# Order of the bank moves, interleaved row ranges and a second DMA queue in a fused attention schedule

## The chip, the cores and the metric

The program runs on one core of one Trainium2 chip. It is a whole decoder of twelve sub-layers in one launch; the metric is the device time of that launch in microseconds. The core's engines are PE (TensorE, matrix products into PSUM), DVE (VectorE), ACT (ScalarE), POOL (GpSimd) and SP (SyncE, which here only issues DMAs). Each runs its own instruction stream in order, and semaphores tie the streams together.

## The reference

Only one of the twelve sub-layers matters here, the fourth layer's attention. It handles 16 batches of 128 rows, width 128, 16 heads of 8, and has two attentions one after the other: each batch over itself, then its output over two fixed sets of 256 past states, which all batches share.

```python
q, k, v = (_split_heads(_lin(hidden_states, W, b)) for W, b in ((Wq, bq), (Wk, bk), (Wv, bv)))
attn = softmax(einsum('bhsd,bhtd->bhst', q, k) * SCALE)
output = _lin(_merge_heads(einsum('bhst,bhtd->bhsd', attn, v)), Wo, bo)
rq = _split_heads(_lin(output, Wrq, brq))
rk = _split_heads(_lin(past_states, Wrk, brk)); rv = _split_heads(_lin(past_states, Wrv, brv))
rattn = softmax(einsum('bhsd,pbhtd->pbhst', rq, rk) * SCALE)
recursive_output = _merge_heads(einsum('pbhst,pbhtd->pbhsd', rattn, rv)).mean(axis=0)
gate = sigmoid(_lin(concatenate([output, recursive_output]), Wg, bg))
return output * (1 - gate) + recursive_output * gate      # then x = layernorm(x + this)
```

All of it is computed in fp32; a fp32 product is two passes on PE, and the trace has one record for each pass.

## The kernel before

`l3_attn` (from line 810) holds the stage. The 16 batches are cut into four groups of `G = 4`, so that a tile is 128 partitions by 512 columns (4 batches by 128). Heads have only 8 rows, so queries and keys of four heads lie in one tile at partitions 0, 32, 64 and 96 (`ROW = 32`), in four such sets (`SETS = 4`). Projections give a dense tile (`dense_q`, `dense_k`, `dense_rk`), and `spread_rows` (line 908) copies its 16 heads of 8 rows, one DMA each, to their places; all these DMAs are issued by SP, in the order of its stream: parameter loads first, then four for `b_rq4`, eight that zero rows of `rk4`, then for each task of kind `q`, `k` or `rk` a wait for its move and 16 copies.

The order of the work is written out by hand in **slots**. A group has 40 (`PER`), and functions say what slot t holds:

- `a_at(t)`: two heads of **scores** (rows are queries), whose maximum DVE takes (`peak`). Slots 8 to 15 of a group hold self scores of the next group (L960, four 128-column products a head, 8 passes), the others past scores (L967, one 512-column product, 2 passes).
- `b_at(t)`: two heads of **turned scores** (rows are keys), 11 slots later, with the maximum folded in as an extra row; ACT takes their exponential (`exp`, L1092). Self ones are L982, past ones L990.
- `o_at(t)`: in every second slot the **values** of four heads, L1004 and L1009, which go to four column ranges of bank 6.
- `misc_at(t)`: at most one **extra task**, always in bank 7, named by a key: `x` and `pt` (turn the input), `q`, `k`, `v`, `rk`, `rv` (projections), `mt` and `rmt` (turn the maxima), `ot` and `rot` (turn the sums for the division), `o2`, `out`, `rq` (output projection and next queries), `rec`, `gate`, `fin` (combine, gate, residual).

PE's stream goes through the slots: a, b, o, misc. Scores use banks 0 to 2 in turn, turned scores banks 3 to 5. `score` (line 941) waits with `pe.wait_ge(maxed, n - 2)` before head n, that is for the reduction of head n - 3; `turned_score` (line 969) waits likewise on `exped`. Each handles one head; for a self head it runs its four batches one after the other in one 32-row range. `other(key)` waits until the previous task's bank has been moved (`moved`).

ACT and DVE each move some kinds of tasks (`ON_ACT` lists ACT's). In slot t both do this, with `exp` on ACT and `peak` on DVE:

```python
two, before = b_at(t), misc_at(t - 1)
if two:
    exp(two[0])
if before is not None and before[0] in ON_ACT:
    evacuate(before)
if two:
    exp(two[1])
```

so the move of the task of slot t - 1 stands between slot t's two exponentials (reductions). Behind them ACT copies a finished sum (`move_sum`, L1099) and scales the result four slots after `fin` (`apply`, L1137); DVE has `blend` after `gate` (L1200 to L1202) and `moments` two slots after `fin` (L1207, L1211). POOL clears tiles, waits for all 15 parameter loads, spreads `w_rq4`, and then computes the layer norm's `rstd` for each group. The first `q` task on PE waits for all 15 loads too.

Since the first scores need queries and keys of group 0 and nothing else can run yet, the stage starts with a stretch that has few tasks in flight (slots -40 to -1); slots 0 to 10 have scores but no turned scores.

## Time and profile before

| | us |
|---|---|
| median of the runs (6590.18 to 6593.02, 3 runs) | 6592.16 |
| the profiled execution | 6582.25 |
| its span, first to last instruction | 6580.5 |
| this stage in it, about 5282 to 5891 | 609 |
| busy in the span: PE 4913.6, DVE 4375.5, ACT 2893.6, POOL 2329.9 | |

A time of a row is the start in the profiled span, then the length. Matmuls are pipelined: a group's busy time reaches from its first start to its last end, and the next group may start a little before that end. The profile gives PE's granted clock as a share of 2.4 GHz: 1.00 is 2.4 GHz, 0.50 is 1.2 GHz. Slots don't appear in the profile; they are found by counting the passes of L960 and L967 in order.

### The profile page before, as it was taken

The numbers are of one execution on the slowest core, as the hardware profiler recorded it, in microseconds if no ns is written. First come the engines' busy times: TensorE is split into PE (matmuls) and PEld (weight loads), VectorE is DVE, ScalarE is ACT, GpSimd is POOL, SyncE is SP. The second block draws the span as 40 slices with busy tenths as digits, with TensorE's granted clock in tenths as the row PEclk, the third lists the DMA queues.
The fourth block names the chain that finished last, engine by engine and source line by source line (L and its number), as shares of the span: only waits on it lengthen the run. The fifth ranks groups of instructions, "written<-read, shape, count | busy, mean of one in ns | idle before, by whom it ended". The sixth has DMA issues, their size and how long they took to land. (4 is left out here: it accounts for less than half of the span.)

```text
span 6580.5 us, 86052 instructions
## 1 busy us (share of the span) xinstructions
PE 4913.6 (75%) x27787; PEld 2961.6 (45%) x27787; DVE 4375.5 (66%) x8424; ACT 2893.6 (44%) x4778; POOL 2329.9 (35%) x2032
## 2 busy tenths in 40 slices
PE   6645799999999999676731667666687678863667
PEld 4534466666666666324521222222465354422434
DVE  4522788888888888474446699999554335538635
ACT  2211577777777776452211455454232314432311
POOL 0011666666666666241011466666100200000100
PEclk8755999999999999787765899999898869985878
DMA  0000100000000000000000000000000000002000
GB/s 13 0 4 0 32 1 18 1 18 1 18 1 18 1 4 1 4 0 2 2 0 0 7 0 0 0 1 0 12 0 12 0 15 5 3 10 54 6 21 6
DMA packets 72547, 48.55 MB, mean 7 GB/s; under 512 B 26672, under 2 KB 66761, under 8 KB 71433
## 3 DMA queue, kind: packets, MB, share of 16 engines
q1 hardware_dynamic: 72201, 44.17, 2.7%
q8 instruction: 189, 3.10, 0.2%
q14 instruction: 157, 1.29, 0.1%
HBM read 39.53 MB, written 1.18 MB: 6 GB/s over the span
## 5 line engine op out<-in xcount | busy, mean ns | idle before, releaser
L2942 POOL TENSOR_TENSOR l_attn_read<-l_attn_state,l_attn_c_rows 128x1024 f32<-128x1024 f32 x256 | 604.4, 2361 | 328.7 <-DVE l_attn_state L2845 327.8
L1828 POOL TENSOR_TENSOR l_ffn_t<-l_ffn_t 128x512 f32<-128x512 f32 x384 | 488.7, 1273 | 593.7 <-DVE l_ffn_t L1696 593.7
L2845 DVE TENSOR_TENSOR_SCAN l_attn_state<-l_attn_decay,psum 128x1024 f32<-128x1024 f32 x256 | 584.9, 2285 | 8.0
L203 POOL TENSOR_SCALAR rstd<-mean_var 128x4 f32<-128x4 f32 (+1 forms) x36 | 8.4, 232 | 1621.4 <-DVE mean_var L192 1621.4
L1428 PE MATMUL psum<-l_ffn_wq,l_ffn_xsT 128*128 128x512 f32 x1152 | 563.2, 597 | 21.9 <-DVE l_ffn_t L1696 13.2
L2647 PE MATMUL psum<-l_attn_read,ident 128*128 128x512 f32 x1024 | 493.9, 605 | 5.4 <-DVE l_attn_yz L2853 3.0
L2638 PE MATMUL psum<-l_attn_parts,pick 96*128 96x512 bf16 x512 | 199.9, 393 | 311.1 <-DVE psum L2837 311.1
L1839 POOL TENSOR_TENSOR l_ffn_p<-l_ffn_p,l_ffn_sm 128x512 f32<-128x512 f32 x384 | 399.8, 1041 | 63.4 <-DVE l_ffn_sm L1728 46.8
L1834 POOL TENSOR_TENSOR l_ffn_t<-l_ffn_t,l_ffn_ss 128x512 f32<-128x512 f32 x384 | 401.0, 1044 | 0.7 <-DVE l_ffn_ss L1711 0.7
L2764 ACT COPY l_attn_c_rows<-psum 128x512 f32<-128x512 f32 x256 | 149.9, 586 | 467.8 <-PE psum L2638 467.7
L1593 ACT COPY l_ffn_pT<-psum 128x512 f32<-128x512 f32 x384 | 224.6, 585 | 271.3 <-PE psum L1458 267.8
L2837 DVE TENSOR_TENSOR psum<-psum,l_attn_du 128x1024 f32<-128x1024 f32 x256 | 315.6, 1233 | 31.7 <-POOL l_attn_du L2919 4.6
L1692 DVE TENSOR_TENSOR l_ffn_t<-psum,l_ffn_tab 128x512 f32<-128x512 f32 x384 | 263.2, 685 | 105.9 <-ACT l_ffn_sq L1576 104.1
L1092 ACT ACTIVATE l_attn_pT<-psum 128x512 f32<-128x512 f32 x320 | 178.3, 596 | 299.2 <-PE psum L990 205.2
L1587 ACT ACTIVATE l_ffn_p<-l_ffn_p 128x512 f32<-128x512 f32 x384 | 241.4, 629 | 150.3 <-DVE l_ffn_p L1719 148.0
L1715 DVE TENSOR_REDUCE l_ffn_mx<-psum 128x4 f32<-128x512 f32 x384 | 257.7, 671 | 73.4 <-PE psum L1449 72.4
L2638 PEld LDWEIGHTS psum<-l_attn_parts,pick 96*128 96x128 bf16 x512 | 49.8, 98 | 555.5 <-DVE psum L2837 483.0
L2757 ACT ACTIVATE l_attn_decay<-l_attn_dt,l_attn_a 128x1016 f32<-128x1016 f32 x256 | 292.8, 1144 | 12.4 <-DVE l_attn_state L2845 12.1
L1472 PEld LDWEIGHTS psum<-l_ffn_pT,l_ffn_v 128*64 128x64 f32 x3072 | 160.1, 136 | 280.2 <-issue 173.8
L1576 ACT ACTIVATE l_ffn_sq<-psum 128x512 f32<-128x512 f32 x384 | 230.6, 601 | 117.0 <-PE psum L1428 117.0
L1173 DVE TENSOR_REDUCE l_attn_rtop<-psum 128x2 f32<-128x512 f32 x256 | 168.7, 685 | 169.8 <-PE psum L967 169.6
L1449 PE MATMUL psum<-l_ffn_kT,l_ffn_qT 64*128 64x128 f32 x3072 | 274.7, 297 | 0.0
(762 smaller groups left out, 12273.6 us busy)
## 6 DMA issues: line engine op xcount, KB each, us to landing
l_ffn_wq<-in_L_ffn_Wqkv SPq DMA_DIRECT2D x6, 1536.0 KB, 6.1
l_xattn_toep<-s4d_taps SPq DMA_DIRECT2D x4, 2048.0 KB, 17.5
l_ffn_wo<-in_L_ffn_Wo SPq DMA_DIRECT2D x6, 512.0 KB, 7.7
l_ffn_w<-in_L_ffn_W SPq DMA_DIRECT2D x6, 341.0 KB
l_ffn_w<-in_L_ffn_w SPq DMA_DIRECT2D x3, 512.0 KB, 5.6
l_attn_q<-l_attn_dense_q SPq DMA_DIRECT2D x64, 16.0 KB
l_attn_k<-l_attn_dense_k SPq DMA_DIRECT2D x64, 16.0 KB
l_xattn_conv_y<-l_xattn_conv_rows SPq DMA_DIRECT2D x64, 16.0 KB, 2.2
```

The costliest lines, as they stand in the source:

```text
L1428: nc.tensor.matmul(ring[it % 2], xsT[:, n % 2, m % G, :], wq[:, z, i * 512:(i + 1) * 512], start=True, stop=True).then_inc(itemed, 1)
L1449: last = nc.tensor.matmul(S[:, par, i, :], qT[r, m % G, 2 * c + i, :], kT[r, m % G, 2 * c + i, :], start=False, stop=True, skip_group_chec ...
L1692: nc.vector.tensor_tensor(t1[:, m % G, i, :].rearrange("p (h d) -> p h d", d=dh), dots.rearrange("p (h d) -> p h d", d=dh), rows(tab[:, z, ...
L1715: nc.vector.reduce_max(mx[:, k % 2, :, :], S, AX).then_inc(max_found, 1)
L1828: nc.gpsimd.tensor_tensor(t1[:, m % G, i, :], t1[:, m % G, i, :], t2[:, x % 3, :], ALU.add).then_inc(added, 1)
L1834: nc.gpsimd.tensor_tensor(t1[:, m % G, i, :].rearrange("p (h d) -> p h d", d=dh), t1[:, m % G, i, :].rearrange("p (h d) -> p h d", d=dh), ...
L1839: nc.gpsimd.tensor_tensor(p_[:, k % 4, :, :], p_[:, k % 4, :, :], col(sm[:, k % 4, :], T), ALU.mult).then_inc(weighted, 1)
L2647: last = nc.tensor.matmul(total[:, h * GT:(h + 1) * GT], K.ident[:], read[:, k % 3, h * GT:(h + 1) * GT], start=(n == 0), stop=(n == N - 1 ...
L2757: nc.scalar.activation(decay[:, k % 3, :, :, 1:T], dt[:, g % 2, :].rearrange("p (h g t) -> p h g t", h=2, g=G)[:, :, :, 1:T], ACT.Exp, sca ...
L2837: nc.vector.tensor_tensor(drive.rearrange("p (h n) -> p h n", h=2), rows(b_bank, 2), du[:, g % 2, :].rearrange("p (h n) -> p h n", h=2), A ...
L2845: nc.vector.tensor_tensor_scan(state[:, k % 3, :], decay[:, k % 3, :, :, :].rearrange("p h g t -> p (h g t)"), drive, 0.0, ALU.mult, ALU.a ...
L2942: nc.gpsimd.tensor_tensor(read[:, k % 3, :].rearrange("p (h n) -> p h n", h=2), state[:, k % 3, :].rearrange("p (h n) -> p h n", h=2), row ...
```

## The change

1. In ACT's and DVE's slots the move of the previous slot's task comes first, ahead of both exponentials or reductions.
2. `score` and `turned_score` take both heads of the slot. They wait for both banks first. For self heads the loop over batches is outside and the loop over the two heads (two row ranges, two banks) inside.
3. Weights and biases of q and k are loaded first, on a semaphore `qk_in` of their own, for which the first q task waits; the wait for the other 11 loads moves to the `rk` task.
4. The 16 copies of a `k` task are issued by POOL instead of SP. POOL's stream goes through the slots, too: for group 0 the copies stand ahead of the `w_rq4` spread, for the others at the slot of their task, between the `rstd` computations.

```diff
-            N_LOAD = 15
+            N_LOAD = 11
+            def spread_rows(eng, dst, src, sem):
+                for s in range(SETS):
+                    for j in range(4):
+                        h = 4 * j + s
+                        eng.dma_start(dst[ROW * j:ROW * j + dh, s, :], src[dh * h:dh * h + dh, :]).then_inc(sem, 16)
...
-                    for n in ("q", "k", "v", "rk", "rv", "o", "rq"):
+                    for n in ("q", "k"):
+                        sp.dma_start(w[n][:], I[pre + "W" + n]).then_inc(qk_in, 16)
+                        sp.dma_start(bias[n][:], column(I[pre + "b" + n])).then_inc(qk_in, 16)
+                    for n in ("rk", "v", "rv", "o", "rq"):
                         sp.dma_start(w[n][:], I[pre + "W" + n]).then_inc(loaded, 16)
...
-                    if key[0] == "k":
-                        spread_rows(k4, stage_k, k_set)
...
-                def score(key):
-                    n = a_use[key]
-                    if n >= 3:
-                        pe.wait_ge(maxed, n - 2)
+                def score(keys):
+                    for key in keys:
+                        n = a_use[key]
+                        if n >= 3:
+                            pe.wait_ge(maxed, n - 2)
...
                         for b in range(G):
                             at = slice(b * T, b * T + T)
-                            last = nc.tensor.matmul(ps[:, at], q4[r, s, at], k4[r, s, at], start=True, stop=True)
+                            for j in (j0, j0 + 1):
+                                r = slice(ROW * j, ROW * j + ROW)
+                                ps = K.bank[a_use["self", g, s, j] % 3]
+                                last = nc.tensor.matmul(ps[:, at], q4[r, s, at], k4[r, s, at], start=True, stop=True)
+                                if b == G - 1:
+                                    last.then_inc(a_done, 1)
...
                     if kind == "q":
                         if g == 0:
-                            pe.wait_ge(loaded, 16 * N_LOAD)
+                            pe.wait_ge(qk_in, 64)
...
                     if kind == "rk":
+                        pe.wait_ge(loaded, 16 * N_LOAD)
...
                     two, before = b_at(t), misc_at(t - 1)
-                    if two:
-                        exp(two[0])
                     if before is not None and before[0] in ON_ACT:
...
                         evacuate(before)
-                    if two:
-                        exp(two[1])
+                    for key in two:
+                        exp(key)
...
+                def spread_k(key):
+                    pool.wait_ge(moved, use[key] + 1)
+                    spread_rows(nc.gpsimd, k4, stage_k, k_set)
...
+                pool.wait_ge(cleared, 2)
+                spread_k(("k", 0))
+                pool.wait_ge(loaded, 16 * N_LOAD)
+                pool.wait_ge(rq_bias, 64)
...
+                for t in slots:
+                    key, done = misc_at(t), misc_at(t - 2)
+                    if key is not None and key[0] == "k" and key[1] > 0:
+                        spread_k(key)
+                    if done is not None and done[0] == "fin":
+                        rstd_of(done[1])
```

`turned_score` is changed as `score` is, and DVE's slots as ACT's.

## Rows read from the trace of the kernel before

**Rows 1.** By stretch: length, busy PE, PEld, DVE, ACT, POOL (instructions), PEclk, DMA, GB/s.

```profile
5554.00:5678.00 124.00, 107.93 (x916) 55.66 (x917) 65.84 (x125) 58.06 (x110) 1.67 (x4) 1.00 0.03 5
...
5400.00:5440.00 40.00, 40.00 (x193) 27.27 (x191) 17.77 (x27) 5.43 (x10) 0.00 (x0) 0.50 0.00 1
5441.00:5812.00 371.00, 325.94 (x2642) 158.96 (x2634) 195.61 (x374) 174.15 (x325) 3.42 (x9) 1.00 0.02 4
```

**Rows 2.** Timeline of an odd slot with task rq: PE, then ACT.

```profile
5625.48 0.70 PE L967 MATMUL psum<-l_attn_rk,l_attn_rq 32*128 32x512 f32 x2
...
5627.95 1.12 PE L1059 MATMUL psum<-l_attn_outT,l_attn_w_rq 128*128 128x512 f32 x2 [1.33 <-ACT l_attn_rq L1119]
5629.01 0.70 PE L967 MATMUL psum<-l_attn_rk,l_attn_rq 32*128 32x512 f32 x2
...
5626.72 0.60 ACT L1092 ACTIVATE l_attn_pT<-psum 128x512 f32<-128x512 f32 x1 [1.39 <-PE psum L990]
5627.22 0.68 ACT L1119 ACTIVATE l_attn_rq<-psum,l_attn_b_rq 128x512 f32<-128x512 f32 x1
```

**Rows 3.** Timeline of PE, the even slot before it.

```profile
5621.95 0.70 PE L967 MATMUL psum<-l_attn_rk,l_attn_rq 32*128 32x512 f32 x2
...
5623.02 1.06 PE L1009 MATMUL psum<-l_attn_pT,l_attn_rv 128*32 128x512 f32 x8
5624.42 1.12 PE L1059 MATMUL psum<-l_attn_outT,l_attn_w_rq 128*128 128x512 f32 x2 [0.34 <-ACT l_attn_rq L1119]
```

**Rows 4.** Timeline of PE, an odd and an even slot without a task.

```profile
5519.05 0.70 PE L967 MATMUL psum<-l_attn_rk,l_attn_rq 32*128 32x512 f32 x2
...
5520.96 0.70 PE L990 MATMUL psum<-l_attn_rq,l_attn_rk 32*128 32x512 f32 x2
...
5522.02 1.06 PE L1009 MATMUL psum<-l_attn_pT,l_attn_rv 128*32 128x512 f32 x8
5523.02 0.70 PE L967 MATMUL psum<-l_attn_rk,l_attn_rq 32*128 32x512 f32 x2
```

**Rows 5.** Timeline of PE, a slot with self scores; and self values.

```profile
5541.59 1.37 PE L960 MATMUL psum<-l_attn_k,l_attn_q 32*128 32x128 f32 x13
5542.70 0.70 PE L990 MATMUL psum<-l_attn_rq,l_attn_rk 32*128 32x512 f32 x2
...
5543.75 1.07 PE L1009 MATMUL psum<-l_attn_pT,l_attn_rv 128*32 128x512 f32 x8
...
5377.87 1.08 PE L1004 MATMUL psum<-l_attn_pT,l_attn_v 128*32 128x128 f32 x32
```

**Rows 6.** Timeline of PE: a task of four turns, and rec.

```profile
5589.04 0.66 PE L1015 MATMUL psum<-ident,l_attn_rtop 128*128 128x128 f32 x4 [0.67 <-DVE l_attn_o L1195]
...
5556.76 2.05 PE L1063 MATMUL psum<-ident,l_attn_ro 128*128 128x128 f32 x16 [0.36 <-DVE l_attn_q L1184]
```

**Rows 7.** Timeline of the start: copies issued by SP, and the first scores.

```profile
5296.55 10.71 SPq L913 DMA_DIRECT2D l_attn_q<-l_attn_dense_q  x16
5307.31 11.04 SPq L913 DMA_DIRECT2D l_attn_k<-l_attn_dense_k  x16
...
5319.83 9.18 PE L960 MATMUL psum<-l_attn_k,l_attn_q 32*128 32x128 f32 x64 [13.53 <-DMA l_attn_k<-l_attn_dense_k]
```

**Rows 8.** Timeline of PE: first scores of slots 12, 16, 56, 80 and 96.

```profile
5418.63 0.58 PE L960 MATMUL psum<-l_attn_k,l_attn_q 32*128 32x128 f32 x1
...
5438.48 1.22 PE L967 MATMUL psum<-l_attn_rk,l_attn_rq 32*128 32x512 f32 x2
...
5554.26 0.70 PE L967 MATMUL psum<-l_attn_rk,l_attn_rq 32*128 32x512 f32 x2
...
5635.51 0.70 PE L967 MATMUL psum<-l_attn_rk,l_attn_rq 32*128 32x512 f32 x2
...
5677.54 0.70 PE L967 MATMUL psum<-l_attn_rk,l_attn_rq 32*128 32x512 f32 x2
```

**Rows 9.** Timeline of DVE, slots with scores alone.

```profile
5394.64 2.60 DVE L1173 TENSOR_REDUCE l_attn_rtop<-psum 128x2 f32<-128x512 f32 x4 [11.22 <-PE psum L967]
```

More of the change, by code:

```diff
@@ L897, in l3_attn @@
         ON_ACT = ("x", "q", "k", "rq", "pt", "rk", "o2", "out", "rec", "gate", "fin")
-        names = ("past_in", "loaded", "spread", "cleared", "clear_step", "zeroed", "filled", "moved", "q_set", "k_set", "rk_set", "rq_bias",
+        names = ("past_in", "qk_in", "loaded", "spread", "cleared", "clear_step", "zeroed", "filled", "moved", "q_set", "k_set", "rk_set", "rq_bias",
                  "a_done", "maxed", "b_done", "exped", "o_done", "o_moved", "recip", "mix_step", "mixed", "stats_step", "var_ready", "rstd_step",
@@ L959, in score @@
                             at = slice(b * T, b * T + T)
-                            last = nc.tensor.matmul(ps[:, at], q4[r, s, at], k4[r, s, at], start=True, stop=True)
-                    else:
-                        _, g, s, b, j = key
-                        r = slice(ROW * j, ROW * j + ROW)
-                        if b == j == 0:
-                            pe.wait_ge(moved, use["rq", g, s] + 1)
-                            pe.wait_ge(rk_set, 256)
-                        last = nc.tensor.matmul(ps, rq4[r, g % 2, s, b * T:b * T + T], rk4[r, s, :], start=True, stop=True)
@@ L968, in score @@
-                    last.then_inc(a_done, 1)
-                def turned_score(key):
-                    n = b_use[key]
-                    if n >= 3:
-                        pe.wait_ge(exped, n - 2)
-                    ps = K.bank[3 + n % 3]
-                    if key[0] == "self":
-                        _, g, s, j = key
-                        r = slice(ROW * j, ROW * j + ROW)
-                        if j == 0:
+                            for j in (j0, j0 + 1):
[4 more added lines that the diff above has]
+                                    last.then_inc(a_done, 1)
+                    else:
+                        for key in keys:
+                            _, g, s, b, j = key
+                            r = slice(ROW * j, ROW * j + ROW)
+                            if b == j == 0:
+                                pe.wait_ge(moved, use["rq", g, s] + 1)
+                                pe.wait_ge(rk_set, 256)
+                            nc.tensor.matmul(K.bank[a_use[key] % 3], rq4[r, g % 2, s, b * T:b * T + T], rk4[r, s, :],
+                                             start=True, stop=True).then_inc(a_done, 1)
@@ L979, in turned_score @@
+                def turned_score(keys):
+                    for key in keys:
+                        n = b_use[key]
+                        if n >= 3:
+                            pe.wait_ge(exped, n - 2)
+                    if keys[0][0] == "self":
+                        _, g, s, j0 = keys[0]
+                        if j0 == 0:
                             pe.wait_ge(moved, use["mt", g, s] + 1)
@@ L981, in turned_score @@
                             at = slice(b * T, b * T + T)
-                            last = nc.tensor.matmul(ps[:, at], k4[r, s, at], q10[r, s, at], start=True, stop=True)
-                    else:
-                        _, g, s, p, kb, j = key
-                        r = slice(ROW * j, ROW * j + ROW)
-                        if p == kb == j == 0:
-                            pe.wait_ge(moved, use["rmt", g, s] + 1)
-                            pe.wait_ge(zeroed, 128)
-                        at = (2 * p + kb) * T
-                        last = nc.tensor.matmul(ps, rk4[r, s, at:at + T], rq10[r, s, :], start=True, stop=True)
-                    last.then_inc(b_done, 1)
+                            for j in (j0, j0 + 1):
+                                r = slice(ROW * j, ROW * j + ROW)
+                                ps = K.bank[3 + b_use["self", g, s, j] % 3]
+                                last = nc.tensor.matmul(ps[:, at], k4[r, s, at], q10[r, s, at], start=True, stop=True)
+                                if b == G - 1:
+                                    last.then_inc(b_done, 1)
+                    else:
+                        for key in keys:
+                            _, g, s, p, kb, j = key
+                            r = slice(ROW * j, ROW * j + ROW)
+                            if p == kb == j == 0:
+                                pe.wait_ge(moved, use["rmt", g, s] + 1)
+                                pe.wait_ge(zeroed, 128)
+                            at = (2 * p + kb) * T
+                            nc.tensor.matmul(K.bank[3 + b_use[key] % 3], rk4[r, s, at:at + T], rq10[r, s, :], start=True, stop=True).then_inc(b_done, 1)
                 def value(key):
@@ L1075, in _ @@
                 for t in slots:
-                    for key in a_at(t):
-                        score(key)
-                    for key in b_at(t):
-                        turned_score(key)
+                    if a_at(t):
+                        score(a_at(t))
+                    if b_at(t):
+                        turned_score(b_at(t))
                     if o_at(t) is not None:
@@ L1219, in _ @@
                     two, before = a_at(t), misc_at(t - 1)
-                    if two:
-                        peak(two[0])
                     if before is not None and before[0] not in ON_ACT:
                         evacuate(before)
-                    if two:
-                        peak(two[1])
+                    for key in two:
+                        peak(key)
                     if before is not None and before[0] == "gate":
```

38 lines of the change are left out of this document (14 added, 24 removed).

## The prediction

> **What bounds the kernel now.** The change touches one stage, the fourth layer's attention, about 5282 to 5891 us of a span of 6580.5. I read the busy time by stretch first [rows 1]. No engine is full: between 5554 and 5678, the 124 us in which group 1 runs in full, PE is busy 108, DVE 66 and ACT 58. So waits and PE's order decide. PE's timeline cut into slots of the hand-written schedule comes next (a slot starts with the first L967 or L960 matmul). A group has 40 slots; that one takes 5554.26 to 5677.54, 123.28 us [rows 8].
>
> An odd slot (two rows of score heads, two of turned scores, one extra task) shows the wait [rows 2]: scores start at 5625.48, the task's matmul only at 5627.95, 2.47 later, and the next slot at 5629.01. ACT explains it. It takes the first exponential at 5626.72, when the scores are ready, and only then moves the previous task's bank at 5627.22 for 0.68; the single task bank is free at 5627.90, and PE goes on at 5627.95. That bank was full 2.4 us before. PE stood idle 1.33 of this.
>
> An even slot also has values [rows 3]: scores 5621.95, values 5623.02, task 5624.42, next slot 5625.48, 3.53 in all; the values hide most of the same wait. Without a task [rows 4] the odd and even slots together take 5519.05 to 5523.02, 3.97, and another limit appears: three banks per kind. The even slot's second head waits for the odd slot's first reduction and starts at 5520.96, 1.91 after the slot before.
>
> **Part 1: the move ahead of both reductions or exponentials.** It adds and removes no instruction. Prices: from scores to another kind of matmul 1.06 (5520.96 to 5522.02), values 1.00 (5522.02 to 5523.02) [rows 4]; a task of two 512-column passes 1.06 (5627.95 to 5629.01) [rows 2]; four turns are busy 0.66 [rows 6], less the 0.07 by which the next start overlaps (as 1.12 busy against 1.06 in rows 2): 0.59; rec 1.99 likewise from 2.05 [rows 6], and gate and fin, which are as long, 1.93. The move itself is 0.68 and starts once the earlier task has drained, so it ends near 0.8 to 1.2 after the slot's start, beside the scores: at nothing on the path. What is late next: PE itself, or the three banks. So an odd slot with a task becomes the larger of 1.06 + task and 1.90; an even one 1.06 + 1.00 + task.
>
> Group 1, its first 24 slots, now 5554.26 to 5635.51 = 81.25 [rows 8]. New, odd: four with turns 4 x 1.90 = 7.6 (1.65 by PE, the banks rule); five with two passes 5 x 2.12 = 10.6; v 2.15; gate 2.99; fin 3.94 (DVE's three blend operations, 0.7 each, follow gate's move and both reductions, and fin waits for them). Sum 27.3. Even: nine with turns 9 x 2.65 = 23.9; two with passes 2 x 3.12 = 6.2; rec 4.05; 0.3 more where DVE's moments or ACT's four scalings get in front of a reduction. Sum 34.5. Together 61.8: a gain of 19.5.
>
> **Part 2: row ranges alternate.** Today a self head's eight passes run in one row range, one behind the other, at 0.11 apart: in [rows 5] L960 runs from 5541.59, and the other kind's scores, queued behind both heads, start only at 5542.70, 1.11 later; values follow at 5543.75, so 2.16 after the start. Would two ranges really run side by side? L1004 already alternates over four column ranges: 32 passes in 1.08 us [rows 5], where one range at 0.11 would need 3.5. L967 and L990 start four heads in four ranges together. So I take full overlap: the block falls by one head's 0.55, to about 1.61, wherever the bank wait isn't the limit. In the remaining 16 slots of group 1, 5635.51 to 5677.54, nine have no task, or one that hides (gain 0.2, since odd and even still add up to 3.97), and seven have the group's first kind as self scores: 5 x 0.55 + 2 x 0.81 (part 1 helps there too) = 4.4. In the eight slots where the turned scores are self scores, part 2 shortens the even slots by 0.55 each; that is already in the 2.65. Group 1: 19.5 + 0.2 + 4.4 = 24.
>
> The same prices for the 5438 to 5554 stretch (slots without rec, gate, fin): 20.6. For 5678 to 5768 (32 slots, fewer tasks as no group follows): 14.0.
>
> **The added wait.** A pair now waits for both heads' banks before either starts. Where a slot has both kinds or values this costs nothing: PE's order made the rest wait already. Where only one kind runs, the pair can't overlap the reduction before it. DVE alone now runs four reductions in 2.60 [rows 9], 1.30 a slot; the new slot is 1.90 at the full clock, and about 2.9 at half. Eight such slots at 5393 to 5405, now 11.9, become 15.2 to 19.2: I take +5. Eight with self scores at 5320 to 5343 cost about +0.65 each without a task (2.70 for 2.04) and lose as much less where a turn's wait goes: +0.1 in sum. Turned scores at 5344 to 5370 gain 1.9, the serial tasks after them 0.4, slots 8 to 15 of group 0 gain 3.2 (some 15 matmuls of it still at half clock, [rows 1], 5400 to 5440). Start region: -0.4. After 5768, one kind only: exponentials set the pace (unchanged); gate and a few tasks give 2.
>
> **Part 3: loads first, keys by POOL.** Today q's sixteen copies are issued from 5296.55, k's behind them from 5307.31, the last lands about 1.5 after its issue ended, and the first scores start at 5319.83 after 13.5 idle [rows 7]. The earlier semaphore lets q's matmul start at about 5287 instead of 5292.8, but SP still has the same loads and eight rk rows in front, so q's copies still start at 5296.55 and land by 5308.8. k's bank is moved by about 5292.9, and POOL is free by then. No row shows a copy issued by POOL. Bounds: SP's 0.67 each (10.71/16), and for the other end twice that, 1.34, as a second engine that forms each copy itself has no row here. I take 1.0, the middle: 5293 + 16 + 1.5 = 5310.4, a gain of 9.4, call it 9. At 0.67 the q copies rule: 11.1; at 1.34: 4.0. Later groups' keys have 20 slots of slack. POOL's rstd work for group g stands six slots ahead of a key spread and isn't delayed; rk's copies leave SP 11 us earlier and are needed 75 us later.
> The Trainium skill speaks partly against this ("DMA: Bandwidth & Descriptors", Issuing engines are not separate DMA queues): a second issuing engine saves only the sequencer's time, since all copies share the same DMA engines. Here SP's issue, 10.7 us for sixteen copies, is the long part, so by that rule the gain would stand too; had the transfers been the limit, the term would be 0. The same page (Latency and other measured facts) gives about 1 us to the first byte for GpSimd-issued copies; if each issue cost that, 16 us, an estimate that agrees with the middle and isn't its ground.
>
> **Sum.** -9 -0.4 -20.6 -24 -14 -2 = -70.0 us. Against the profiled execution's 6582.25: 6512. The median of the runs is 9.9 above it, 6592.16, and I subtract from that: **6522 us**.
>
> **Rivals.**
> *Second bank.* If PE in effect waits for a slot's second reduction or exponential too (moves push both back), an odd slot is not 1.90 but about 2.45. For: ACT already spends 0.68 + 0.49 + 0.60 in such a slot. Against: the wait counts name the first. About 60 odd slots x 0.45 = 27 less: 6549. 12%.
> *Alternation gives nothing.* Weight loads of two ranges queue up. Against: L1004. Costs 0.55 in some 45 slots, 24: 6546. 9%.
> *POOL slow.* 2 us a copy: keys land at 5326.5, 6.7 later than now, not 9 earlier: 6538. 9%.
> *Slower: the clock.* PE's granted clock was 0.50 in 5400 to 5440 and 1.00 from then on, with four row ranges busy [rows 1]. Should the one-kind slots with their longer pauses keep it at 1.2 GHz, each later slot costs more: four slots (12 to 15 of a group) take 5418.63 to 5438.48, 19.9 us, in group 0 at half clock [rows 8] and 5541.59 to 5554.26, 12.7, in group 1 [rows 5, 8]: 1.8 a slot. It turns the sum from the 39th such slot on; for two groups (80 slots) +144 - 70: 6666. Against: PE's pauses become shorter in every slot that had a task. 4%. In the other direction the denser slots may lift it earlier, worth up to 10.
> *Not what it says*, the bank not being the limit: then nothing moves and the one-kind slots add 5: about 6590. 2%.
>
> **How the numbers follow.** The forecast case has 64%. Its own spread: POOL -2/+5, one-kind slots and clock +/-5, slot prices 15% of 59 (+/-9): 6508 to 6540. The range reaches to the first two rivals: 6505 to 6556. A measurement of this kernel can tell about 0.2%, 13 us, from no change. Faster by more: 0.95; within: 0.02; slower: 0.03.
>
> **What would show it.** After: the group from its slot 16 to the next takes 99 us, not 123; in odd slots the task matmul follows the scores at 1.06, and ACT's move stands before the slot's first exponential; PE waits for ACT's rq hardly at all; self passes of two ranges start in pairs 0.11 apart; the first scores start near 5310; DVE's reductions at 5393 to 5405 have 0.6 gaps. The prediction is wrong if odd slots stay near 2.5, if the POOL copies take over 1.3 us each, or if the clock row of 5441 to 5812 falls below 1.00.

## Result and profile after

The changed kernel took **6533.49 us** (median of 4 runs, 6525.79 to 6540.53) against 6592.15: a ratio of 0.9914, 95% interval 0.9899 to 0.9929. The prediction was 6522, range 6505 to 6556. The profiled execution took 6532.18, its span 6530.4, 50.1 less than the span of before. The medians lie 58.7 apart: the profiled run of before was 9.9 below its median, that of after 1.3. So the steps are compared between the two profiles, by stretch.

By stretch, kernel after, from the stage's first load over slots -32, 0, 16, 56, 96, 128 and 169 to ACT's last instruction of the stage, the next stage's first load and the end (columns as in [rows 1]):

```profile
5283.48:5309.73 26.25, 12.54 (x30) 6.49 (x31) 8.67 (x8) 4.51 (x6) 14.86 (x26) 0.50 0.27 59
5309.73:5381.72 71.99, 58.04 (x446) 42.27 (x446) 15.68 (x29) 16.28 (x28) 8.00 (x16) 0.63 0.07 12
5381.72:5431.19 49.47, 41.07 (x206) 21.07 (x205) 22.60 (x35) 5.98 (x11) 0.00 (x0) 0.56 0.00 1
5431.19:5529.17 97.98, 92.58 (x879) 42.93 (x879) 63.30 (x113) 54.63 (x101) 7.95 (x16) 0.98 0.04 7
5529.17:5630.14 100.97, 96.50 (x910) 46.49 (x909) 66.62 (x125) 58.08 (x109) 9.77 (x20) 1.00 0.03 7
5630.14:5710.58 80.44, 72.92 (x678) 34.14 (x677) 52.64 (x101) 47.15 (x89) 1.67 (x4) 1.00 0.01 1
5710.58:5811.06 100.48, 84.79 (x443) 28.08 (x443) 41.48 (x80) 44.03 (x82) 1.66 (x4) 0.90 0.00 1
5811.06:5837.60 26.54, 14.52 (x66) 6.96 (x62) 4.73 (x15) 6.99 (x14) 1.66 (x4) 0.81 0.00 0
5837.60:5843.20 5.60, 0.00 (x0) 0.00 (x0) 0.00 (x0) 0.00 (x0) 0.00 (x0) 0.50 0.01 1
5843.20:6530.43 687.23, 394.62 (x2569) 259.19 (x2570) 402.52 (x1569) 155.07 (x302) 46.05 (x76) 0.74 0.10 23
```

PE is now busy 96.50 of group 1's 100.97 us; it was 107 of 123. The same cut through before, and through one of the experiments (E4, below), gives this ledger. "Predicted" is the prediction's own term.

| stretch | before | after | change | predicted | E4 |
|---|---|---|---|---|---|
| first load to slot -32 | 37.42 | 26.25 | -11.2 | -9 | 26.24 |
| slots -32 to 15 | 118.65 | 121.46 | +2.8 | -0.4 | 116.75 |
| slots 16 to 55 | 115.78 | 97.98 | -17.8 | -20.6 | 95.54 |
| slots 56 to 95 (group 1) | 123.28 | 100.97 | -22.3 | -24 | 99.53 |
| slots 96 to 127 | 91.15 | 80.44 | -10.7 | -14 | 77.50 |
| slots 128 to 168 | 97.33 | 100.48 | +3.2 | -2 | 97.33 |
| **stage to slot 169** | 583.61 | 527.58 | **-56.0** | -70.0 | 512.89 |
| slot 169 to ACT's last | 24.97 | 26.54 | +1.6 | 0 | 23.40 |
| change of stage | 2.41 | 5.60 | **+3.2** | 0 | 5.59 |
| the stages behind | 687.12 | 687.23 | +0.1 | 0 | 691.38 |
| the stages ahead | 5282.41 | 5283.48 | +1.1 | 0 | 5285.30 |

**An odd slot with rq**, timeline of PE, then ACT; it answers to [rows 2]:

```profile
5585.06 0.70 PE L973 MATMUL psum<-l_attn_rk,l_attn_rq 32*128 32x512 f32 x2
...
5586.13 1.13 PE L1070 MATMUL psum<-l_attn_outT,l_attn_w_rq 128*128 128x512 f32 x2
5587.19 0.70 PE L973 MATMUL psum<-l_attn_rk,l_attn_rq 32*128 32x512 f32 x2
...
5585.17 0.69 ACT L1130 ACTIVATE l_attn_rq<-psum,l_attn_b_rq 128x512 f32<-128x512 f32 x1 [0.42 <-PE psum L1070]
5586.30 1.08 ACT L1103 ACTIVATE l_attn_pT<-psum 128x512 f32<-128x512 f32 x2 [0.45 <-PE psum L1001]
```

The move starts 0.11 after the slot and the exponentials follow. The task comes 1.07 behind the scores, with no wait, and the slot takes 2.13 where it took 3.53.

**A slot with self scores**, PE; it answers to the first group of [rows 5]:

```profile
5612.30 0.82 PE L963 MATMUL psum<-l_attn_k,l_attn_q 32*128 32x128 f32 x10
5612.86 0.70 PE L1001 MATMUL psum<-l_attn_rq,l_attn_rk 32*128 32x512 f32 x2
...
5613.92 0.66 PE L1025 MATMUL psum<-ident,l_attn_rtop 128*128 128x128 f32 x4
5614.50 0.38 PE L963 MATMUL psum<-l_attn_k,l_attn_q 32*128 32x128 f32 x2
```

Turned scores start 0.56 after the self scores, not 1.11.

**Slots with one kind** (0 to 4), PE, then DVE; they answer to [rows 9]:

```profile
5381.72 1.13 PE L973 MATMUL psum<-l_attn_rk,l_attn_rq 32*128 32x512 f32 x4
5383.72 1.13 PE L973 MATMUL psum<-l_attn_rk,l_attn_rq 32*128 32x512 f32 x4 [0.87 <-DVE l_attn_rtop L1182]
...
5387.65 2.08 PE L973 MATMUL psum<-l_attn_rk,l_attn_rq 32*128 32x512 f32 x4 [0.84 <-DVE l_attn_rtop L1182]
5390.56 2.07 PE L973 MATMUL psum<-l_attn_rk,l_attn_rq 32*128 32x512 f32 x4 [0.83 <-DVE l_attn_rtop L1182]
...
5382.88 1.29 DVE L1182 TENSOR_REDUCE l_attn_rtop<-psum 128x2 f32<-128x512 f32 x2 [11.21 <-PE psum L973]
5384.85 1.29 DVE L1182 TENSOR_REDUCE l_attn_rtop<-psum 128x2 f32<-128x512 f32 x2 [0.68 <-PE psum L973]
```

PE and DVE take turns: each slot waits 0.85 for DVE, and DVE waits 0.68 for PE. The first slots, at 2.4 GHz, take 2.0 us, those from 5387.65 on, at 1.2 GHz, 2.91; there DVE waits 1.62.

**The start**, SP's queue, POOL and PE; it answers to [rows 7]:

```profile
5297.63 10.71 SPq L911 DMA_DIRECT2D l_attn_q<-l_attn_dense_q  x16
...
5294.60 8.25 POOL L911 DMA_DIRECT2D l_attn_k<-l_attn_dense_k  x16 [5.34 <-ACT l_attn_dense_k L1116]
...
5309.73 2.08 PE L963 MATMUL psum<-l_attn_k,l_attn_q 32*128 32x128 f32 x16 [6.70 <-DMA l_attn_q<-l_attn_dense_q]
```

POOL issues a copy in about 0.5 us (8.25/16), faster than SP in 0.67. Its last copy is issued by 5302.85 and a copy lands 1.8 us after its issue, so the keys are there by 5305 or so; the queries are now last.

### The profile page after: what moved, and what is told of

It reads as the page before. It is cut to its first block and busy times, and to the rows that moved or that the text cites. A ratio compares the mean times of both kernels' runs of the same rounds, so it can differ in the third digit from the quotient of the medians.

```text
span 6530.4 us, 86354 instructions
## 1 busy us (share of the span) xinstructions
PE 4875.4 (75%) x27785; PEld 2919.0 (45%) x27787; DVE 4377.8 (67%) x8424; ACT 2893.0 (44%) x4778; POOL 2359.2 (36%) x2096
## 5 line engine op out<-in xcount | busy, mean ns | idle before, releaser
L1448 PE MATMUL psum<-l_ffn_wq,l_ffn_xsT 128*128 128x512 f32 x1152 | 564.9, 599 | 20.5 <-DVE l_ffn_t L1716 12.0
L2777 ACT ACTIVATE l_attn_decay<-l_attn_dt,l_attn_a 128x1016 f32<-128x1016 f32 x256 | 292.8, 1144 | 11.5 <-DVE l_attn_state L2865 11.1
L2658 PEld LDWEIGHTS psum<-l_attn_parts,pick 96*128 96x128 bf16 x512 | 50.1, 98 | 552.8 <-DVE psum L2857 480.3
L1739 DVE TENSOR_TENSOR l_ffn_p<-psum,l_ffn_mx 128x512 f32<-128x512 f32 x384 | 265.4, 691 | 13.2
```

What stands on the lines that cost most here:

```text
L1448: nc.tensor.matmul(ring[it % 2], xsT[:, n % 2, m % G, :], wq[:, z, i * 512:(i + 1) * 512], start=True, stop=True).then_inc(itemed, 1)
L1739: nc.vector.tensor_tensor(p_[:, k % 4, :, :].rearrange("p (i par) t -> p par i t", par=2), S, mx[:, k % 2, :, :].unsqueeze(3).to_broadcast ...
L2777: nc.scalar.activation(decay[:, k % 3, :, :, 1:T], dt[:, g % 2, :].rearrange("p (h g t) -> p h g t", h=2, g=G)[:, :, :, 1:T], ACT.Exp, sca ...
```

## Experiments

All runs in one table; "stage" is the length from the first load to slot 169 in the profile, which compares kernels better than a total does (E11, E12).

| kernel | median us | ratio to before | 95% interval | stage |
|---|---|---|---|---|
| after | 6533.49 | 0.9914 | 0.9899 to 0.9929 | 527.6 |
| E1 moves between | 6592.32 | 1.0002 | 0.9993 to 1.0011 | 583.1 |
| E2 moves first, alone | 6546.85 | 0.9934 | 0.9921 to 0.9948 | 543.5 |
| E3 heads in series | 6567.10 | 0.9970 | 0.9959 to 0.9982 | 561.1 |
| E4 late waits | 6520.69 | 0.9892 | 0.9876 to 0.9907 | 512.9 |
| E5 keys by SP | 6552.06 | 0.9941 | 0.9928 to 0.9955 | 541.1 |
| E6 like E4, zero rows late | 6513.57 | 0.9889 | 0.9874 to 0.9904 | 502.3 |
| E7 like E6, with fillers | 6509.79 | 0.9878 | 0.9863 to 0.9893 | 505.2 |
| E8 start alone | 6585.15 | 0.9998 | 0.9989 to 1.0007 | 576.3 |
| E9 one-kind slots late | 6523.20 | 0.9902 | 0.9886 to 0.9917 | 523.7 |
| E10 like E6, half the filler | 6526.49 | 0.9912 | 0.9899 to 0.9926 | 523.1 |
| E11 before again (1 run) | 6583.90 | | | 586.8 |
| E12 after again (1 run) | 6536.49 | | | 527.6 |

### E1: alternation and start, the moves back between

```diff
-                    if before is not None and before[0] in ON_ACT:
-                        ...
-                    for key in two:
-                        exp(key)
+                    if two:
+                        exp(two[0])
+                    if before is not None and before[0] in ON_ACT:
+                        ...
+                    if two:
+                        exp(two[1])
```
(and the same on DVE)

> The changed kernel with part 1 undone: the task's move stands again between the slot's two exponentials (reductions). Pairs, alternation, early loads and POOL's key copies stay. Theory (the bank of the task is the limit): in odd slots the task matmul again follows the scores by about 2.4 us instead of 1.07, group 1 (its slot 16 to the next group's) takes about 118.5 us instead of the changed kernel's 101.0, and the time is about 6580 us. Rival (the alternation carries the gain, the moves little): group 1 below 108 us and a time near 6550.

Measured: 6592.32, no change in the total, where the theory had 6580. Group 1 takes 120.89 us, near the theory's 118.5 and far from the rival's 108. Slot 77, PE, then ACT and DVE:

```profile
5619.46 0.70 PE L973 MATMUL psum<-l_attn_rk,l_attn_rq 32*128 32x512 f32 x2
...
5621.93 1.13 PE L1070 MATMUL psum<-l_attn_outT,l_attn_w_rq 128*128 128x512 f32 x2 [1.33 <-DVE l_attn_rtop L1184]
...
5620.71 0.60 ACT L1103 ACTIVATE l_attn_pT<-psum 128x512 f32<-128x512 f32 x1 [1.39 <-PE psum L1001]
5621.20 0.68 ACT L1130 ACTIVATE l_attn_rq<-psum,l_attn_b_rq 128x512 f32<-128x512 f32 x1
...
5620.62 1.29 DVE L1184 TENSOR_REDUCE l_attn_rtop<-psum 128x2 f32<-128x512 f32 x2 [2.24 <-PE psum L973]
```

The picture of [rows 2] is back to the hundredth: task 2.47 behind the scores, 1.33 idle. (The profile names DVE, whose reductions end at 5621.91. By the code the task waits for the move alone, which ends at 5621.88; the two lie 0.03 apart.)

The total hides gains and losses. Alternation gives its 0.55 also here wherever the slot doesn't wait for the move. Slot 90, PE:

```profile
5652.34 0.83 PE L963 MATMUL psum<-l_attn_k,l_attn_q 32*128 32x128 f32 x10
5652.90 0.70 PE L1001 MATMUL psum<-l_attn_rq,l_attn_rk 32*128 32x512 f32 x2
...
5655.54 0.83 PE L963 MATMUL psum<-l_attn_k,l_attn_q 32*128 32x128 f32 x10
```

It takes 3.20 us for 3.75 in before, while slots 56 to 67, where the move decides, gain 0.5 us in all. Slots 16 to 95 together gain 4.0 us, and the start has its 11.2 us too. Against that stand 2.8 us in slots -32 to 15, 2.0 in slots 96 to 127, and 9.9 in slots 128 to 168 (107.22 for 97.33), where the granted clock was 0.84 for 0.93. So the stage ends 0.5 us shorter than before's, and the change of stage and the stages behind take 7.3 us more. Where a slot waits for the move, time saved in front of it is worth nothing; in the other slots it counts.

### E2: the moves first, alone

The kernel before with this on ACT, the same on DVE, and nothing else:

```diff
-                    if two:
-                        exp(two[0])
                     if before is not None and before[0] in ON_ACT:
                         ...
-                    if two:
-                        exp(two[1])
+                    for key in two:
+                        exp(key)
```

> The kernel before with part 1 alone: the task's move first, everything else as before. Theory: odd slots with four turns near 1.9 to 2.0, with a two-pass task near 2.15, self slots still with heads in series; group 1 about 108.5 us (before 123.3), nothing gained at the start, one-kind slots as before: about 6553 us. Rival (without the alternation the freed slots run into the three banks again): group 1 above 115 and a time above 6570.

Measured: 6546.85, 6 us below the theory. Group 1 by stretch:

```profile
5544.03:5650.52 106.49, 106.49 (x910) 56.15 (x909) 66.85 (x124) 58.58 (x109) 1.67 (x4) 1.00 0.03 6
```

That is 16.8 of the 22.3 us that group 1 gained, and 40.1 of the stage's 56.0: the largest part by far. Odd slots with turns and past scores (57, 71 and 73) take 1.66 here, not the 1.9 to 2.0 of the theory. Of the other 15.9 us of the stage the start has 11.1, so alternation and the pair waits together are worth some 4.8; with the late waits of E4 the same difference is some 19.

### E3: heads in series again

```diff
-                        for b in range(G):
-                            at = slice(b * T, b * T + T)
-                            for j in (j0, j0 + 1):
+                        for j in (j0, j0 + 1):
+                            for b in range(G):
+                                at = slice(b * T, b * T + T)
```

> The changed kernel with the two loops exchanged: a pair of self heads still waits for both banks first, but runs head after head. Theory: each slot with self scores and another kind is 0.55 us longer at the full clock (a self slot of group 1 about 2.76 and 3.75 instead of 2.21 and 3.20), one-kind self slots are not longer (2.7 to 2.9 at half clock, since the first head's reduction starts earlier), in sum +22: about 6555. Rival (alternation gives nothing): within 4 us of the changed kernel's 6533.

Measured: 6567.10, slower than the theory said. Slot 89, PE, to be laid beside the self slot of after:

```profile
5640.70 1.37 PE L963 MATMUL psum<-l_attn_k,l_attn_q 32*128 32x128 f32 x13
5641.81 0.70 PE L1001 MATMUL psum<-l_attn_rq,l_attn_rk 32*128 32x512 f32 x2
...
5643.46 0.37 PE L963 MATMUL psum<-l_attn_k,l_attn_q 32*128 32x128 f32 x1
```

1.11 again in place of 0.56, and 2.76 us for the slot in place of 2.20: the 0.55 of the prediction, so two row ranges do run side by side. The Trainium skill ("TensorEngine Tiling (Array Packing)", Key Properties) says that different tiles can run weight loads and matmuls in parallel; the trace agrees. Group 1 takes 108.47, 7.5 more than after. The slots -32 to 15 take 135.0 for 121.5. As expected, slots with self scores alone and no task are not longer (2.9 us in both kernels); but those with a task are (slots -29 and -27: 4.04 for 3.05), and so are the turned ones with a task (slot -20: 4.07 for 3.05), mostly at 1.2 GHz. That the expectation had left out. Slots 128 to 168 take 4.5 us more, with 34 us at 1.2 GHz in place of 20.5.

### E4: each wait in front of its own multiplication

```diff
-                    for key in keys:
-                        n = a_use[key]
-                        if n >= 3:
-                            pe.wait_ge(maxed, n - 2)
+                    def free(key):
+                        n = a_use[key]
+                        if n >= 3:
+                            pe.wait_ge(maxed, n - 2)
+                    ...
+                            if alone and b == 0:
+                                free(keys[j - j0])
...
                         for key in keys:
+                            free(key)
```
(`alone`: the slot holds one kind; its self heads then run in series. Self heads beside the other kind alternate and wait in pairs as in after. `turned_score` likewise)

> The changed kernel, but each past head waits for its own bank only, right ahead of its own matmul, and a self pair is alternated (with both waits first) only in slots that hold the other kind too; alone it runs head after head with its own wait. Theory (the early wait costs the one-kind slots): the eight slots from slot 0 of group 0 take about 12 us instead of 20.5, the eight self slots at the start about 2 less, the ones near the end 2 to 3 less: about 6521. Rival (the clock decides there: PE is granted half clock whenever only one kind runs, and what the waits give back it takes): 6528 to 6538, with as much time at half clock as the changed kernel.

Measured: 6520.69, the time that was expected, and better than both kernels, but in part by another way: the theory had no gain in slots 16 to 127, and these give 6.8 of the stage's 14.7 us, while the stages behind took 4.2 us more. A slot without a task and the next one, PE:

```profile
5592.44 0.70 PE L980 MATMUL psum<-l_attn_rk,l_attn_rq 32*128 32x512 f32 x2
...
5593.41 1.62 PE L980 MATMUL psum<-l_attn_rk,l_attn_rq 32*128 32x512 f32 x3
...
5596.40 0.70 PE L980 MATMUL psum<-l_attn_rk,l_attn_rq 32*128 32x512 f32 x2
```

and the same two slots in the kernel after:

```profile
5598.79 0.70 PE L973 MATMUL psum<-l_attn_rk,l_attn_rq 32*128 32x512 f32 x2
...
5600.79 0.70 PE L973 MATMUL psum<-l_attn_rk,l_attn_rq 32*128 32x512 f32 x2 [0.85 <-DVE l_attn_rtop L1182]
...
5602.97 0.70 PE L973 MATMUL psum<-l_attn_rk,l_attn_rq 32*128 32x512 f32 x2
```

In the kernel before, the first head of the even slot of [rows 4] started 0.98 after the odd slot (5519.05):

```profile
5520.03 1.62 PE L967 MATMUL psum<-l_attn_rk,l_attn_rq 32*128 32x512 f32 x3
```

With late waits it starts 0.97 after, and the two slots take 3.96; with the pair wait it starts 2.00 after and the two take 4.18. An odd slot with turns takes 1.66 instead of 2.00. The ledger's last column says what that adds up to: each of the middle stretches has, to within 0.4 us, the length that the prediction's term gave it.

### E5: the keys by SP again

```diff
+                    if key[0] == "k":
+                        sp.wait_ge(moved, use[key] + 1)
+                        spread_rows(sp, k4, stage_k, k_set)
...
-                spread_k(("k", 0))
...
-                    if key is not None and key[0] == "k" and key[1] > 0:
-                        spread_k(key)
```

> The kernel after, with the sixteen copies of group 0's keys (and the later groups') issued by SP again behind those of the queries; the earlier loads, the moves and the alternation stay. In the kernel after POOL issues a copy every 0.50 us beside SP's 0.67. Theory (the queue is what the start gains by): the keys' copies follow the queries' on one queue, sixteen times 0.67 = 10.7 us later, and the first scores with them: from the stage's first load to slot -32 about 37 us in place of 26.3, and the time about 6533 + 10.7 = 6544 us. Rival (the earlier loads give the start's gain and the queue nothing): 26 to 28 us to slot -32 and 6533 to 6535 us.

Measured: 6552.06, 8 us above the theory; slot -32 is 37.41 us behind the first load, as the theory said. SP's queue, and by stretch the start and the change of stage:

```profile
5301.37 10.71 SPq L911 DMA_DIRECT2D l_attn_q<-l_attn_dense_q  x16
5312.13 11.01 SPq L911 DMA_DIRECT2D l_attn_k<-l_attn_dense_k  x16
```

```profile
5287.21:5324.62 37.41, 12.53 (x31) 6.52 (x31) 8.67 (x8) 4.52 (x6) 6.63 (x10) 0.50 0.19 42
...
5854.90:5857.37 2.47, 0.00 (x0) 0.00 (x0) 0.00 (x0) 0.00 (x1) 0.00 (x0) 0.50 0.02 7
```

So without the second queue the earlier loads give nothing: they only let q's matmul run sooner, ahead of copies that can't start sooner. Whether the queue would give the 11.2 us without them was not run. The time above the theory is not in the start: slots -32 to -1 took 2.2 us more than in after, and the stages behind 6.6 us more (693.81), in the same code. And the second row gives a price that the prediction did not have: the change of stage takes 2.47 us here and 5.60 in after.

### E6: the zero rows behind the queries

```diff
-                for j in range(4):
-                    for p in range(2):
-                        ...
...
                         spread_rows(sp, q4, stage_q, q_set)
+                        if key[1] == 0:
+                            zero_rows()
```
(against E4; `zero_rows` holds the loop that is taken out, the eight copies into `rk4`)

> The kernel with each wait in front of its own slot's first multiplication (e4_late_waits), and the eight copies of zero rows, which SP issues ahead of the queries' copies, moved behind the first set of those. Theory (SP's queue decides when the first scores start, since they wait for the queries' copies): eight times 0.67 = 5.3 us less in front of slot -32, 21 us from the stage's first load in place of 26.3, and the time about 6520.7 - 5 = 6516 us. Rival (the copies wait for the projections and not for their queue): slot -32 where it was, and 6520 to 6521 us.

Measured: 6513.57. SP's queue and PE:

```profile
5296.04 10.84 SPq L911 DMA_DIRECT2D l_attn_q<-l_attn_dense_q  x16
...
5308.53 9.21 PE L972 MATMUL psum<-l_attn_k,l_attn_q 32*128 32x128 f32 x64 [1.73 <-DMA l_attn_q<-l_attn_dense_q]
```

Slot -32 is 21.54 us behind the first load, 4.7 earlier than in E4. Its stage of 502.3 us is the shortest of all. Of the 10.6 us that it is shorter than E4's, 4.6 lie in slots -32 to 15, whose code is the same, with 86 us at 1.2 GHz in place of 96.

### E7 and E10: fillers for the clock

E7 adds to E6, in slots -32 to 15 without a task:

```diff
+                    elif -32 <= t < 16:
+                        pe.wait_ge(moved, ...)
+                        for _ in range(2):
+                            nc.tensor.matmul(misc, K.ident16[:], K.zeros16[:], start=True, stop=True)
```

E10 has one of them instead of two, and only up to slot -1; so it changes two things against E7.

> e6_late_waits_zero_rows with two multiplications more (128 x 128 by 512 columns, 16 bit, of zeros) in every slot from -32 to 15 that has no task; nothing reads what they write. Theory (the granted clock of PE follows how densely it is used, and the slots -32 to 15 run at half of it for 60 of their 76 us because their score multiplications use little of the array): the clock is granted in full over most of these slots and they take 8 to 20 us less, 6496 to 6508 us. Rival (the clock has its own course there): the granted clock falls and rises where it did and each filler pair costs 0.4 us at full clock and 0.9 us at half, 10 to 35 us more, 6526 to 6550 us.

> e6_late_waits_zero_rows with one filler multiplication in place of two, and only in the slots -32 to -1 that have no task. In e7_filler the granted clock of PE was 1.0 from 5362 us on where e6_late_waits_zero_rows had 0.5 up to 5418 us but for two stretches, and the fillers took back what that gave. Theory (half as much filler still keeps the clock up): 1.0 from about 5362 us on, slots -32 to -22 6 us longer than without filler in place of 12, slots 8 to 15 at 18.5 us in place of 27, 6500 to 6506 us. Rival (half of it is too little, or it has to go on up to slot 15): the clock is 0.5 again in the slots 0 to 15, and the filler only costs, 6514 to 6525 us.

Slots 0 to 15 by stretch, of E6, E7 and E10:

```profile
5381.55:5420.68 39.13, 38.36 (x205) 23.91 (x205) 22.92 (x35) 5.52 (x10) 0.00 (x0) 0.61 0.00 1
```

```profile
5391.94:5424.42 32.48, 32.48 (x230) 16.14 (x229) 22.15 (x35) 5.52 (x10) 0.00 (x0) 1.00 0.00 1
```

```profile
5392.86:5434.23 41.37, 40.60 (x206) 25.35 (x205) 23.06 (x35) 5.98 (x11) 0.00 (x0) 0.57 0.00 1
```

With two fillers a slot (E7) the granted clock is 1.00 over these slots, without any (E6) 0.61, and in E10, where the single fillers end at slot -1, 0.57. So the clock follows what PE is given to do there; it doesn't have a course of its own. But the fillers cost 12.3 us in slots -32 to -22 alone (36.63 for 24.30), at 1.2 GHz, and slots -32 to 15 take 117.2 us for 112.2: the clock came as the theory said, the 8 to 20 us did not. The stage is 3 us longer than E6's, and the time, 6509.79, lies just above the theory's range and can't be told apart from E6's. (The theory's 60 of 76 us at half clock were those of slots -32 to -1 in E4.) E10's fillers cost 17.6 us up to slot 0 (90.57 for 73.02) and buy nothing: the rival's case, with 6526.49 us just above its 6514 to 6525. Whether one filler would do if it went on up to slot 15 is open.

### E8: the start alone

The kernel before with parts 3 and 4 of the change:

```diff
+                    for n in ("q", "k"):
+                        sp.dma_start(w[n][:], I[pre + "W" + n]).then_inc(qk_in, 16)
...
+                spread_k(("k", 0))
```

> The kernel before with the start's parts of the change alone: W and b of q and k loaded ahead of the rest, and the keys' copies issued by POOL. Score multiplications and moves stay as before. Theory (the start is worth 11 us by itself, and the alternation and the pair waits take back what it gives in the kernel with the moves between): from the stage's first load to slot -32 26.3 us in place of 37.4, every later stretch as before, the time 6592 - 11 = 6581 us. Rival (what comes earlier at the start is waited for later in any case, by the clock or by the tasks): 6587 to 6592 us, as in the kernel with the moves between.

Measured: slot -32 at 26.26, the 11.2 us are there; the time, 6585.15, can't be told from before. The rival is nearer: what comes earlier is spent later. By stretch, the stage to slot 169 and the change of stage:

```profile
5281.07:5857.40 576.33, 505.99 (x3585) 268.38 (x3585) 268.16 (x488) 229.69 (x422) 43.89 (x86) 0.87 0.03 7
...
5882.27:5887.87 5.60, 0.00 (x0) 0.00 (x0) 0.00 (x0) 0.00 (x1) 0.00 (x0) 0.50 0.01 1
```

Of the 11.2 us, 3.9 go within the stage (-32 to 15 take 120.7 for 118.7, with 100 us at 1.2 GHz in place of 95; slots 16 to 55 116.9 for 115.8, with 4.7 in place of 2.4), 3.2 at the change of stage. The stages behind took 691.3 us for 687.1, in code that is the same. Over all fourteen profiles that same code took 684.2 to 693.8 us, so part of what a total shows comes from there.

**The change of stage** is a step function over all fourteen profiles: 2.41 to 2.47 us in the four in which only SP issues the stage's DMAs (before, E11, E2, E5), 5.59 to 5.60 in the ten in which POOL does as well, whatever else differs. E5 and after differ in this alone. No record says what fills the gap; that it goes with POOL's copies is shown, what POOL does in it is open.

### E9: late waits in slots with one kind only

```diff
-                    if keys[0][0] == "self" and not alone:
+                    if not alone:
                         for key in keys:
                             free(key)
...
-                            free(key)
+                            if alone:
+                                free(key)
```
(against E4)

> The kernel after, with one thing changed in the slots that hold scores of one kind (-32 to 7): their multiplications run one head after the other, each behind its own wait. Slots with both kinds wait for both banks first, as in the kernel after. In e4_late_waits both sorts of slot have the late waits, and it was 12 us faster than the kernel after. Theory (both sorts have a share, by the slots of e4_late_waits: 4.7 us up to slot 16 and 10 us behind it): slots 0 to 7 take 12.1 us in place of 20.5, slots 56 to 95 stay at 101 us, 6528 us. Rival (the slots with one kind account for it all): 6521 us.

Slots 0 to 7 take 12.1 us, group 1 stays at 100.95, slots -32 to 15 take 116.75 as in E4. The theory's shares hold in the profile: 4.7 us up to slot 15, and the stretches 16 to 127 keep 4.9 of the 6.8 us that E4 takes off them. The median, 6523.20, lies between the 6528 of the theory and the rival's 6521, a little nearer the rival's. Against after the stage is 3.9 us shorter (2.8 are lost in slots 128 to 168, with 30.7 us at 1.2 GHz inside instead of 20.5) and slot 169 to ACT's last instruction 3.1 shorter (23.40), 7.0 of the 10.3 us; the stage of 523.7 us against E4's 512.9 speaks against the rival.

### E11 and E12: before and after once more

> The kernel before once more, for a second profile of it. In the kernel with the start's parts alone the stage was 7.3 us shorter than in the kernel before (576.3 for 583.6 us from its first load to slot 169), and what follows the stage 7.3 us longer (721.8 for 714.5), although nothing is changed there. Theory (the granted clock ahead of the stage and behind it is another one in every execution): the stage again takes 583.6 us to within 2, but it starts somewhere between 5279 and 5290 us, and what follows takes 713 to 723 us, by several us other than 5282.4 and 714.5. Rival (every execution of a kernel is alike, and the later stages give the gain back because they start earlier): start, stage and rest within 1 us of 5282.4, 583.6 and 714.5.

> The kernel after once more, for the same question. Theory: the stage takes 527.6 us to within 2 again; its start and what follows it (5283.5 and 719.4 us in the first profile) differ by several us. Rival: all three within 1 us of the first profile.

The theory was wrong in half, and so was the rival. The stage of after took 527.56 us again and the stages behind 687.27 (687.23): equal to 0.1. Before: stage 586.83 for 583.61, the difference in slots 0 to 15 (46.57 for 45.00), 16 to 55 (+0.9) and 128 to 168 (+0.8), where other stretches had 1.2 GHz; group 1, all at 2.4 GHz, 123.29 for 123.28. Change of stage 2.41, stages behind 687.33 for 687.12. Only the stage's start moved, by 4.3 us in after and 1.9 in before. So 3.2 and 1.6 of the 4.9 us given back behind slot 169 belong to the change, not to chance. The totals of these two runs lie 47.4 us apart, their stages 59.3: a total of one run says little here.

## Why the prediction was right, and where it was off

The mechanism and its order of size were right: the wait for the one task bank is gone, the stage takes 527.6 us against 583.6, and E2 shows that the moves alone give 40.1 of the 56.0. Point by point:

**Moves.** "An odd slot with a task becomes the larger of 1.06 + task and 1.90; an even one 1.06 + 1.00 + task": 2.13 with two passes (2.12 predicted), 2.16 for v (2.15), 3.02 and 3.88 for gate and fin (2.99, 3.94), even ones with turns 2.65 to 2.81 (2.65), rec 4.29 (4.05). The first 24 slots of group 1 took 62.80 us, predicted 61.8, before 81.25. *Second bank* didn't come about.

**Alternation.** 0.55 a head pair, measured 0.55 to 0.56 (E3). *Alternation gives nothing* fell. But with the pair wait that came with it, its net in the stage was some 4.8 us (E2).

**The added wait: the step that failed.** "Where a slot has both kinds or values this costs nothing: PE's order made the rest wait already" and "odd and even still add up to 3.97". The even slot's second head had to wait, but its first did not; it used to start 0.98 after the odd slot, and with the pair wait starts 2.00 after. The pair takes 4.18 to 4.32 instead of 3.97, and an odd slot with turns 2.00 instead of 1.66. By E4 this cost 2.4, 1.4 and 2.9 us in the stretches 16 to 55, 56 to 95 and 96 to 127. Without it the three come to -20.2, -23.8 and -13.7 where the prediction had -20.6, -24 and -14: the rest of that sum stands.

**Slots with one kind.** Right in mechanism, too small: slots 0 to 7 took 20.46 for 11.91, +8.6 and not +5. The prediction had 1.90 and 2.9 a slot, which fits (1.97 and 2.91), but its upper end of 19.2 is four slots of each; all eight at 2.9 are 23.2, and five ran at 1.2 GHz. Slots -32 to -22 cost 1.5 more where +0.1 was said: without a task they took 2.85 to 2.95, not 2.70. The turned ones gained 3.2 for 1.9, the serial tasks after them nothing for 0.4, slots 8 to 15 4.1 for 3.2.

**Slots 128 to 168.** -2 predicted, +3.2 measured. "After 5768, one kind only: exponentials set the pace (unchanged)" was read wrongly: slots 139 to 146 hold scores alone, which wait for DVE's reductions, and the pair wait costs there as in slots 0 to 7 (slot 143 takes 1.92 for 0.86). Slots 142 to 151 took 28.27 us for 23.59. By stretch, the kernel before and after:

```profile
5805.66:5829.25 23.59, 21.77 (x78) 9.01 (x78) 13.99 (x29) 6.68 (x13) 1.67 (x4) 0.71 0.00 0
...
5745.89:5774.16 28.27, 21.94 (x78) 6.76 (x77) 14.79 (x31) 7.28 (x15) 1.66 (x4) 0.64 0.00 0
```

Before had 13.7 us at 1.2 GHz in it (5812.9 to 5826.6), after 20.5 (5752.6 to 5773.1). E4 has 20.4 there and takes 25.10: so 3.2 is the pair wait again. The 1.5 that are left go with the longer low stretch; that they are its effect is not shown. The *clock* rival did not come: 5435 to 5752 was at 1.00 throughout.

**Start.** -9 predicted with 1.0 us a copy; POOL took 0.5, better than the prediction's lower bound of 0.67. The gain stopped at the prediction's own limit, "At 0.67 the q copies rule: 11.1", measured 11.2. *POOL slow* fell. The Trainium skill ("DMA: Bandwidth & Descriptors", Issuing engine by pattern) calls the path of sync and scalar generally the faster one; for the issue of these copies the trace shows the opposite, 0.52 (8.25/16) against 0.67.

**Beyond the stage.** The prediction put nothing there. It was +3.2 for the change of stage and +1.6 behind slot 169, of which 1.4 is slot 169 itself waiting for its pair.

Sum of what was missed in the profiled pair: 14.0 in the stage, 4.9 behind it, 1.1 ahead of it that is no effect, 20 in all: 70 predicted, 50 found. That the median came out 11.5 off and not 20 is luck: the profiled run of before lay low against its median.

## What to carry to other kernels

When two operations are put side by side to overlap, keep each one's wait in front of itself: a joint wait in front of both makes the first one late by whatever the second one waits for, and it costs most where there is the least other work. If a single buffer is emptied by an engine that does other things first, the order on that engine is worth more than the work it feeds; until that is fixed, time saved in a slot that waits for it shows nothing (E1, slots 56 to 67). A second engine that issues DMAs should be priced twice, at its issue and at the end of the stage, and such parts are judged by stage lengths in two profiles, not by totals.

## What the runs showed of the hardware

A copy of 16 KB from one on-chip tile to another takes POOL about 0.5 us to issue and SP 0.67. With POOL's copies in a stage, the change to the next took 5.59 to 5.60 us (ten profiles) instead of 2.41 to 2.47 (four). Over slots 0 to 15 of E6 PE's granted clock was 0.61, although PE was busy through 38 of the 39 us; with two fillers in each slot without a task (E7) it was 1.00. The stage of after, profiled twice with the same lengths at 1.2 GHz, took 527.58 and 527.56 us.

Open: what the change of stage waits for; why the stages behind take 684 to 694 us in the same code; whether the keys issued by ACT, which is busy for 4.5 of the start's 26 us, would avoid it (not tried); and fillers that are placed where they cost less.
